# Blocks of zero products ahead of five waits of TensorE in a gated delta rule and mixture-of-experts layer

## What is computed

```python
x = x + attn(layernorm(x)); x = x + ffn(layernorm(x))

# attn: projection, causal convolution over 4 taps and silu, q and k normalised, then for each token
S = S * exp(g_t)
delta = (v_t - k_t @ S) * b_t
S = S + outer(k_t, delta)
o_t = q_t @ S
# y = norm(o) * silu(z), times W_out

# ffn: h = rmsnorm(x); the 4 largest of softmax(h @ router)
# sum of the 4 experts' silu(g) * u products, weighted, plus the shared expert, plus x
```

## Time and profile before

| | |
|---|---|
| median of 3 runs | 1166.93 us |
| profiled execution, its own time | 1162.42 us |
| its span (first to last instruction) | 1160.6 us |
| mean granted TensorE clock | 0.849 of full speed |
| TensorE MATMUL busy | 971.9 us (84%), 12359 records |
| VectorE, ScalarE, GpSimd busy | 60%, 42%, 55% |
| DMA | 165.33 MB, mean 142 GB/s |

### The profile page before, as it was taken

The page is one execution under the profiler, slowest core; times in us unless marked ns, Lnnn a source line. Parts: engine busy times, 40 slices in busy tenths (PEclk is TensorE's granted clock), DMA queues, the critical chain, the costliest instruction groups (busy, mean ns, idle before and its releaser), DMA issues.

```text
span 1160.6 us, 32029 instructions
## 1 busy us (share of the span) xinstructions
PE 971.9 (84%) x12359; PEld 826.5 (71%) x12359; DVE 696.9 (60%) x1703; ACT 489.6 (42%) x932; POOL 641.9 (55%) x783
## 2 busy tenths in 40 slices
PE   4876899989898988999789889974886989999970
PEld 3765788778787878878778877873784657777760
DVE  6378957667765865776585476668443444333338
ACT  5524445345453543545364354531522234444430
POOL 3041348858875885787688578645031115555550
PEclk8686888879778887988997697797778989999995
DMA  6737036649348654933956540111147234444429
GB/s 234 228 77 189 1 69 177 169 115 279 97 127 216 175 170 131 276 103 107 261 129 174 153 98 29 34 39 37 69 202 285 92 96 132 129 131 129 128 47 359
DMA packets 181826, 165.33 MB, mean 142 GB/s; under 512 B 75427, under 2 KB 174124, under 8 KB 180784
## 3 DMA queue, kind: packets, MB, share of 16 engines
q10 hardware_dynamic: 72208, 73.96, 22.5%
q1 hardware_dynamic: 101840, 72.47, 21.3%
q0 software_dynamic: 7632, 16.87, 4.5%
HBM read 65.76 MB, written 101.55 MB: 144 GB/s over the span
## 4 chain that ended last, share of the span: by engine, by line
PE 43%; POOL 15%; DVE 14%; issue 10%; DMA 4%; another core or an unknown queue 2%; ACT 2%; SPq 1%; POOLq 0%; DVEq 0%; ACTq 0%
PE ps L1531 5%; POOL arena L785 5%; POOL arena L782 5%; PE ps L1615 4%; DVE arena L1119 4%; PE ps L1396 3%; POOL nrm L748 3%; PE ps L1548 3%; PE ps L1450 3%; PE ps L1460 3%; PE ps L1606 2%; PE ps L1429 2%; PE ps L1440 2%; PE ps L1406 2%
## 5 line engine op out<-in xcount | busy, mean ns | idle before, releaser
L1119 DVE SCALAR_TENSOR_TENSOR arena<-ps,cw,arena 128x256 f32<-128x256 f32 x384 | 155.4, 475 | 42.8 <-ACT arena L907 42.5
L1396 PE MATMUL ps<-work,arena 128*128 128x259 f32 x512 | 159.7, 469 | 15.4 <-DVE arena L1119 9.2
L1396 PEld LDWEIGHTS ps<-work,arena 128*128 128x128 f32 x512 | 116.5, 236 | 41.7 <-DVE arena L1119 10.4
L837 POOL DMA_INDIRECT picked<-work x95 | 93.4, 984 | 94.8 <-issue 48.7
L826 POOL DMA_INDIRECT slotted<-hr,slots x64 | 63.7, 996 | 102.6 <-DVE slots L1270 86.4
L785 POOL TENSOR_TENSOR arena<-arena 128x31 f32<-128x31 f32 (+15 forms) x186 | 111.1, 597 | 14.6
L1303 DVE TENSOR_TENSOR work<-work,ps 128x128 f32<-128x128 f32 (+1 forms) x111 | 34.0, 307 | 138.7 <-ACT work L1018 113.3
L1615 PE MATMUL ps<-arena,work 128*128 x380 | 101.3, 389 | 6.1 <-issue 5.0
L782 POOL TENSOR_TENSOR arena<-arena 128x31 f32<-128x31 f32 (+15 forms) x186 | 96.0, 516 | 12.4
L907 ACT ACTIVATE arena<-ps,cw 128x256 f32<-128x256 f32 x128 | 58.1, 470 | 76.6 <-PE ps L1396 60.7
L807 POOL TENSOR_TENSOR work<-work,ec 128x512 f32<-128x512 f32 x32 | 33.7, 1053 | 101.7 <-PE ps L1489 82.5
(11 more groups left out here) (224 smaller groups left out, 2262.6 us busy)
## 6 DMA issues: line engine op xcount, KB each, us to landing
slotted<-blank ACTq DMA_DIRECT2D x17, 4128.0 KB, 18.9
arena<-in_w SPq DMA_DIRECT2D x2, 6528.0 KB, 27.3
arena<-tab SPq DMA_DIRECT2D x96, 128.0 KB, 4.0
work<-slotted SPq DMA_DIRECT2D x95, 129.0 KB
arena<-picked SPq DMA_DIRECT2D x16, 512.0 KB, 9.5
work<-tab SPq DMA_DIRECT2D x32, 128.0 KB, 3.7
arena<-in_w_qkv SPq DMA_DIRECT2D x1, 2048.0 KB, 7.5
xin<-in_x SPq DMA_DIRECT2D x16, 128.0 KB, 4.8
```

Of the source, the lines that this page charges most:

```text
L837: g.indirect_dma_start(out=picked, out_offset=bass.IndirectOffsetOnAxis(ap=to, axis=0), in_=yrow[:, j % SLOTS, :], in_offset=None, bounds_ ...
L1119: v.scalar_tensor_tensor(out=acc_, in0=bank_of("proj", p, s_, i)[:, k:k + W2], scalar=cw[:, u, k:k + 1], in1=acc_, op0=ALU.mult, op1=ALU.a ...
L1396: ins = mm(to[:, 0:WX], wqkv[:, k, m:m + P], xt2[:, p % 3, k, :], start=k == 0, stop=k == KD - 1)
```

## The change

Two helpers multiply a block of zeros (the first 128 columns of `blank`, all 0) by the identity, 128 by 128 by 128 in fp32. One adds the result to what stands in the bank, the other writes it as a product of its own into a bank that the item overwrites afterwards. They are called in five places of TensorE's part of the list: 7 products in every pm, 13 in ks for n % 4 == 1, 9 in ku for n % 4 == 2, 8 in au for n % 4 == 0 and 7 in rank for even b. That is 44 for each of the 8 pairs, 352 in all. In rank the call of `turn` moves ahead of the wait on hot_out.

```diff
+            def add_zeros(to, times):
+                for _ in range(times):
+                    mm(to[:, 0:P], blank[:, 0:P], ident, start=False, stop=False)
+
+            def put_zeros(to, times):
+                for _ in range(times):
+                    mm(to[:, 0:P], blank[:, 0:P], ident, start=True, stop=True)
...
                 if name == "pm":
                     p, = ix
                     to = [turn(name, p, k=k) for k in range(2)]
+                    put_zeros(to[0], 7)
                     pe.wait_ge(S["xt_turned"], 2 * p + 2)
...
                 if name == "ks":
                     n, = ix
+                    if n % 4 == 1:
+                        add_zeros(KS, 13)
                     pe.wait_ge(S["kqs_out"], 2 * n + 1)
                     wait(pe, S["s_out"], n)
...
                 if name == "ku":
                     n, = ix
+                    if n % 4 == 2:
+                        add_zeros(QS, 9)
                     pe.wait_ge(S["ue_out"], n + 1)
...
                 if name == "au":
                     n, = ix
+                    if n % 4 == 0:
+                        add_zeros(QS, 8)
                     pe.wait_ge(S["ue_out"], n + 1)
                     pe.wait_ge(S["at_out"], n + 1)
...
                 if name == "rank":
                     b, = ix
+                    to = turn(name, *ix)
+                    if b % 2 == 0:
+                        put_zeros(to, 7)
                     pe.wait_ge(S["hot_out"], b + 1)
-                    to = turn(name, *ix)
                     mm(to[:, 0:E], before_me, cnt[:, 1, :], start=True, stop=False)
```

## The result

The changed kernel took 1204.91 us (median of 4 runs, 1199.52 to 1217.69), the kernel before 1164.17 us beside it (4 runs). The ratio is 1.0342, with a 95% interval of 1.0249 to 1.0435: slower, by about 40 us where 14.5 were forecast, and 4.9 us above the range. The profiled execution after took 1217.69 us, 12.8 above its own median, so the sums over its trace come out higher than the comparison of medians.

The account below looks back on a forecast made before the run. No engine alone was the bound, but TensorE's work and waits were the largest part (43% of the chain). Exposed zeros of 49.0 us less 34.5 of clock return gave +14.5, on 1163.6 us: 1178 us, range 1166 to 1192.

Parts of the forecast that it names:

- pm: Merge: 7 zeros behind the tap's wait, nothing covers them, 13.4 us exposed; clock behind gives 8 back.
- rank: Routing, even b: 7 zeros start after a tap's wait, 8.7 us exposed; clock behind gives 10 back.
- au: First chunk's value product: 8 zeros well placed ahead of its wait, 3.9 us over; clock gives 4.8 back.
- ks: Second chunk's state product: 13 zeros well placed ahead of its wait, 12.6 us over; clock gives 9.7 back.
- ku: Third chunk's update: 9 zeros with hardly a wait, 10.4 us exposed after slack; clock gives 2 back.
- The price of a zero: Each 128-column zero product takes 0.24 us at full clock, about 0.45 at half; all 352 take 84 us.
- tm row: tm's 3.74 us without idle had clock 0.87, falling at its end: sign that 32 by 32 products don't hold it.
- the slack of 5.2 us at lnp: Behind ku, GpSimd's lnp has slack in pairs 0 to 2; 5.2 us of it covers ku's zeros.
- The stalls: Rival, chance 0.10: 1408 added records make TensorE short of instructions more often, 15 us more, 1193 us.
- Clock up throughout: Rival, chance 0.24: zeros carry the clock over pm and ss as well, 29 us more back, 1149 us.
- nothing back: Rival, chance 0.08: the clock returns nothing, so the exposed +49 us stays, 1213 us.
- Most exposed time has slack: Rival, chance 0.14: GpSimd's solve and su's unnamed wait take it up; +14.5 shrinks to about 0, 1164 us.

Follow-up runs that it names:

- only_pm: Only the 7 zero products of each merge (pm) kept from the change, against the kernel before: 1186.41 us, ratio 1.0187.
- pm_ahead: Only pm's seven zero products, put ahead of the wait for its bank, into the states' bank, against the kernel before: 1145.84 us, ratio 0.9953.
- wide: All five blocks with zero products 512 columns wide and a quarter as many, against the kernel before: 1186.19 us, ratio 1.0332.

## Why the prediction was wrong

The direction and the first fault that it named were right, and the size was not: 14.5 us forecast, about 40 measured. Net terms in the order of the prediction, forecast, then the trace after: pm 5.4 and 18.6; rank -1.3 and 1.3; au -0.9 and 6.8 (its return can't be told apart from ks's step); ks 2.9 and 5.4; ku 8.4 and 24.1. These are sums over one execution that was 12.8 us above its median. By the ratios of the single blocks pm costs 21.7 us, rank 1.6, au -4.1, ks 17.9 and ku 8.6: so measured, pm (16.3 more than forecast) and ks (15.0 more) make the miss, and ku was right.

- **The price of a zero was right.** 0.24 us at full clock (1.73 for seven), 0.45 at half (3.1 for seven).
- **pm: the step that failed.** "I take 1.0 x 8 = 8" was forecast as the clock's return behind pm. The change gave 1.3 back, only_pm 0.6. pm_ahead gave 9.5 back with the same zeros: the size was right for zeros that fill the idle, and the prediction had itself shown that these stand behind it. It used that for the exposed time (13.4) and forgot it for the clock. The tm row explains little of it: pm kept 1.00 in all pairs of pm_ahead, and the clock fell behind it, with no idle ahead, in only two of the seven pairs that had a wait. The exposed part came out as 19.9: 1.6 to 2.0 in six pairs, as forecast, and 4.75 and 4.51 in pairs 1 and 3, where the zeros themselves ran at the low clock (3.0 and 3.1 us) and the wait ahead of them had grown from 1.2 to 2.9 and 2.6. The forecast had priced all zeros there at the full clock.
- **rank: the same, half so.** Exposed 15.5 against 8.7. In pairs 3, 4 and 5 the seven zeros started at the low clock after 1.3 us of idle and took 3.15 us. The return, 14.2 in the steps up to the next pm, was above the 10 forecast, and 12.5 of it came behind the blocks of pairs 0, 1 and 2. Part of it can be chance: the unchanged kernel on the third chip is 7.0 shorter in the same steps. Alone, the block is 1.0014: neutral, as forecast.
- **au: small in both.** Its block is 6.8 longer in the trace of the whole and a gain of 4 us alone, where a gain of 0.9 was forecast.
- **ks: right in its mechanism.** 12.6 exposed and 9.7 returned against 15.7 and 10.3, and 2.94 us for the products where 2.9 was forecast. The block alone gives the same picture at its place, 18.2 and 10.3, but costs 10 us more elsewhere in the kernel, for which the sum has no term and the runs no cause. Nor could the prediction know that the wait which it covered belongs to some chips only.
- **ku: right alone, larger in the whole trace.** Of the 30.7 us between the second and the third ku the zeros take 18.4, 9.8 are more "issue" (8.0 to 17.8), 3.2 are other products that ran slower, and 0.6 of other waits went. The next step gives 6.6 back. Alone, the block costs 8.6 us by its ratio, net as forecast. And the trace before has the least "issue" there of all traces, so that kernels without ku's zeros are 5 to 14 us longer in the same step: most of the surplus in the whole is not the zeros' own. Whether the slack of 5.2 us at lnp was used can't be read from these traces.
- **The stalls: a rival that holds in part.** TensorE waited 28 us for "issue" in the trace before and 39 after. In every kernel nearly all of these stalls over 1 us in pairs 1 to 5 fall at places of its own record stream that are some 249 records, or a multiple of that, apart, so that added records move them to other products. There they fall while the large `blank` stores run, but stalls come not only then: 3.17 us and 2.55 us (at 785 and 837 us before) return in every trace after the last of these stores. wide, as slow as the change with 29 us of "issue", shows that this is not the main cause. Its share of the 40 us stays open: it differs between executions, and no kernel without these stores was timed.
- **Clock up throughout** was excluded by the clock, 0.88 where over 0.93 was asked for; **nothing back** as well, since ks and rank gave 24 back, although pm gave next to nothing. **Most exposed time has slack** is excluded by the time.

The Trainium skill (TensorE: Matmul & The Clock Gate, Why this matters for your kernels) says to avoid idle gaps between bursts, and that the clock then stays up. The page speaks of longer gaps than those here. In these traces short ones were enough: in pair 4, 0.54 behind pm with a gap of 1.74 us ahead of it, 0.62 with a gap of 1.24 and zeros, 1.00 where the zeros filled the gap. The other half holds in the main only: with no gap ahead of pm the clock still fell behind it in pairs 3 and 5 of pm_ahead. The prediction held the tm row against that rule and gave it too little weight at pm.

## What to carry to other kernels

Work put in to keep TensorE's clock must stand where the idle is. TensorE waits in order, so filler behind the wait that ends last leaves the idle and lengthens the path by its own length. At pm it then saved next to nothing, at rank about what it cost; ahead of the wait pm's seven products gained 0.3 to 0.5% instead of costing 1.9%. Ask of each block which wait really ends last, how long it is on the chip at hand, and make the filler no longer than that. When you have found that a block misses its gap, strike its cover from the sum, and don't count on the return that a filled gap would give. Before you size a step from one trace, see how much it moves between traces of kernels that don't touch it.

## What was not expected of the hardware

- The first trace, and those of one of three chips, have a wait between TensorE's ku and VectorE's su that nothing in the profile explains, about 3 us in pairs 1 to 5 of the first; those of the two others have none. Two traces of the same kernel differ by 12.6 us with it. What releases su there is open.
- 128 products of 32 x 32 ran at the full clock for 3.76 us in all eight pairs of pm_ahead, with no gap ahead of them; directly behind a gap of 1.2 to 1.6 us their mean was 0.66 to 0.87 (pairs 0 to 6 before).
- Zeros can also cost the clock: in pair 7, which has no gap, the stretch behind pm had 0.68 with them and 1.00 without.
- A stall of "issue" of 4.61 us inside a run of equal products also costs the clock: v behind it took 1.97 us instead of 1.09.
